# Queries and keys of a cosine attention laid out by feature, normed through TensorE, and fetched per head from DRAM

## The reference, cut to what matters

```python
q = (x @ Wq.T).reshape(b, n, H, 2, DH).transpose(0, 2, 3, 1, 4)   # H = 8, DH = 8
k = (x @ Wk.T).reshape(b, n, H, 2, DH).transpose(0, 2, 3, 1, 4)
v = (x @ Wv.T).reshape(b, n, H, 2 * DH).transpose(0, 2, 1, 3)
L1 = einsum('bhnd,bhmd->bhnm', l2norm(q1), l2norm(k1)) * cos_scale
L2 = einsum('bhnd,bhmd->bhnm', l2norm(q2), l2norm(k2)) * cos_scale
G = tanh(delta_gain * (L1 - L2))
A1, A2 = softmax(L1 + G), softmax(L2 - G)
y = einsum('bhnm,bhmd->bhnd', A1 - lambda_full * A2, v)
```

## Time and profile before

| | us |
|---|---|
| median of 3 runs | 758.65 (756.38 to 758.97) |
| the profiled execution | 760.07 |
| its span, first to last instruction | 758.3 |
| TensorE busy | 664.0 (88%) |
| VectorE busy | 553.7 (73%) |
| ScalarE busy | 479.3 (63%) |
| GpSimd busy | 247.4 (33%) |

### The profile page before, as it was taken

The page is one execution under the profiler, slowest core; times in us unless marked ns, Lnnn a source line. Parts: engine busy times, 40 slices in busy tenths (PEclk is TensorE's granted clock), DMA queues, the critical chain, the costliest instruction groups (busy, mean ns, idle before and its releaser), DMA issues.

```text
span 758.3 us, 9794 instructions
## 1 busy us (share of the span) xinstructions
PE 664.0 (88%) x3514; PEld 287.7 (38%) x3514; DVE 553.7 (73%) x1058; ACT 479.3 (63%) x468; POOL 247.4 (33%) x394
## 2 busy tenths in 40 slices
PE   5999899999999888889988888798898787979795
PEld 2577545444454412222222222132232212547264
DVE  5656430605426389999999999999999997687656
ACT  1243433333342489999999999898999898213211
POOL 3601100102013745951378334547713030020001
PEclk9999999999999979999999999999999999989899
DMA  8000200000000111010111010110011130300430
GB/s 308 3 0 2 85 1 0 1 0 1 0 1 0 28 29 29 15 29 16 29 29 28 18 26 15 29 29 15 18 26 29 28 111 10 105 1 14 98 141 28
DMA packets 16752, 26.00 MB, mean 34 GB/s; under 512 B 2496, under 2 KB 7360, under 8 KB 16320
## 3 DMA queue, kind: packets, MB, share of 16 engines
q1 hardware_dynamic: 16704, 25.38, 12.1%
HBM read 15.87 MB, written 1.11 MB: 22 GB/s over the span
## 4 chain that ended last, share of the span: by engine, by line
PE 45%; ACT 22%; DVE 21%; issue 11%; POOL 1%; DMA 0%; POOLq 0%; DVEq 0%; ACTq 0%
ACT w_hh L881 17%; PE ps L590 7%; PE ps L600 7%; DVE hid L1144 5%; DVE hid L1149 5%; PE ps L630 4%; PE ps L538 4%; PE ps L577 4%; PE ps L519 3%; PE ps L639 3%; PE ps L618 2%; ACT probs L850 2%; PE ps L419 2%; PE ps L450 2%; PE ps L562 1%
## 5 line engine op out<-in xcount | busy, mean ns | idle before, releaser
L881 ACT ACTIVATE w_hh<-hid 128x2048 f32<-128x2048 f32 x128 | 249.0, 1945 | 13.2 <-DVE hid L1149 12.8
L519 PE MATMUL ps<-q_s,k_s 128*128 128x512 bf16 (+1 forms) x512 | 168.6, 393 | 25.6 <-DVE hid L1144 23.9
L538 PE MATMUL ps<-w_hh,v_h 128*32 128x512 f32 x1024 | 140.3, 620 | 31.1 <-ACT w_hh L881 28.6
L1149 DVE SCALAR_TENSOR_TENSOR hid<-ps,probs 128x1024 f32<-128x1024 f32 x86 | 104.6, 1217 | 6.5 <-PE ps L519 5.8
L1144 DVE TENSOR_TENSOR hid<-ps,probs 128x1024 f32<-128x1024 f32 x86 | 104.6, 1216 | 4.4 <-ACT w_hh L881 2.2
L519 PE MATMUL ps<-q_w,k_w 64*128 64x512 bf16 x256 | 100.4, 393 | 1.4 <-DVE hid L1149 1.1
L850 ACT ACTIVATE probs<-ps,gain 128x1024 f32<-128x1024 f32 x86 | 98.5, 1146 | 4.5 <-PE ps L519 4.3
L1479 POOL TENSOR_SCALAR rs<-mv 128x4 f32<-128x4 f32 x32 | 7.3, 227 | 249.6 <-DVE mv L960 249.4
L1053 DVE SCALAR_TENSOR_TENSOR hid<-ps,s_b,rot 128x512 f32<-128x512 f32 x16 | 11.9, 750 | 87.1 <-ACT rot L821 87.1
L519 PEld LDWEIGHTS ps<-q_s,k_s 128*128 128x128 bf16 (+1 forms) x512 | 38.4, 95 | 96.9 <-issue 47.3
L519 PEld LDWEIGHTS ps<-q_w,k_w 64*128 64x128 bf16 x256 | 23.6, 93 | 111.8 <-DVE hid L1149 65.0
(11 more groups left out here) (258 smaller groups left out, 1007.2 us busy)
## 6 DMA issues: line engine op xcount, KB each, us to landing
k_w<-k_s SPq DMA_DIRECT2D x32, 128.0 KB, 2.3
q_w<-q_s SPq DMA_DIRECT2D x32, 128.0 KB, 2.3
w_hh<-w_rows SPq DMA_DIRECT2D x4, 1024.0 KB, 9.0
w_hh<-in_b_h SPq DMA_DIRECT2D x2, 1024.0 KB, 8.8
hid<-w_rows SPq DMA_DIRECT2D x2, 1024.0 KB, 5.9
part<-w_rows SPq DMA_DIRECT2D x8, 256.0 KB, 7.0
x_res<-in_x SPq DMA_DIRECT2D x4, 256.0 KB, 6.0
tab<-in_rope SPq DMA_DIRECT2D x1, 1024.0 KB, 6.8
```

The costliest lines, as they stand in the source:

```text
L519: last = mm(ps[:, base + half, :], k_op[rows, u, keys], q_op[rows, u, half * CHUNK:(half + 1) * CHUNK], start=True, stop=True)
L538: last = mm(ps[VW * g4:VW * g4 + VW, 6, :], v_h[:, u, mt, :], ee[:, mt % 2, g4 * CHUNK:(g4 + 1) * CHUNK], start=(mt == 0), stop=(mt == BT ...
L881: A(ee[:, mt % 2, :], zz[:, mt % 2, :], ACT.Exp).then_inc(S["e"], 1)
L1149: v.scalar_tensor_tensor(zz[:, mt % 2, SEQ:2 * SEQ], banks[:, 4 * CHUNK:6 * CHUNK], -1.0, gg[s % 3], ALU.mult, ALU.subtract).then_inc(S["z ...
```

## The change

Queries and keys are now made with features on partitions: `c_raw` is one product of 512 columns with the weights as the stationary side, for q and for k (L614 of the kernel after), and `c_v` makes v as before (L618). Their norms: GpSimd's squares are multiplied on TensorE with a 128x16 matrix of ones per group of eight (`c_sums`, eight products of 16 columns); VectorE or GpSimd takes the inverse roots and spreads each over its eight features (`spread`); TensorE transposes that (`c_scale`, eight transposes), and the factor, now in PSUM, is multiplied to `raw`. The split in three parts stays.

The parts are written to a DRAM tensor `qk_rows` (`send`, 12 DMAs a chunk), ordered so that the 48 rows of one component of a head lie together; and per head 8 DMAs (`load_head`) bring them to `k_s`, `k_w`, `q_s`, `q_w`, both ways round. This takes the place of the spreading, of the turnings "k" and "q", of their copies and of the crossing. The four head tiles are set to zero once. Chunk 2's projection moves from the start of block C into turnings, chunk 3's pieces are fewer and larger. ScalarE runs one exp of one column before the first tanh of block C. `sg_d` of block D has memory of its own.

```diff
+SPECIAL = {(0, 2): ("raw", 0), (0, 5): ("raw", 1), (1, 1): ("v", 0), (1, 3): ("sums", 0), (2, 1): ("scale", 0),
+           (2, 3): ("scale", 1), (3, 1): ("late turn", 0), (3, 3): ("raw", 2), (3, 5): ("raw", 3), (3, 7): ("v", 1),
+           (4, 5): ("sums", 1), (5, 3): ("scale", 2), (5, 5): ("scale", 3),
...
-    if mt == 0 and n < NH - 1:
-        return ("k", n + 1)
-    if mt == 2 and n < NH - 1:
-        return ("q", n + 1)
...
+Q_PARTS = (0, 0, 1, 0, 2, 1)
+K_PARTS = (0, 1, 0, 2, 0, 1)
...
+        qk_rows = nc.dram_tensor("qk_rows", (BATCH, 2, GROUPS, PARTS, DH, SEQ), BF16, kind="Internal").ap()
...
+        def spread(eng):
+
+            wide = [P, P, DH]
+            return eng.tensor_tensor(sq[:].rearrange("p a (n d) -> p (a n) d", d=DH),
+                                     rstd[:].unsqueeze(2).to_broadcast(wide),
+                                     cs_tab[:].rearrange("p a k h c -> p (a k h c)").unsqueeze(2).to_broadcast(wide), ALU.mult)
...
-            for n in range(NH):
-                for kind, src, dst in (("k", k_s, k_w), ("q", q_s, q_w)):
-                    sp.wait_ge(S["turn_read"], turns_done((kind, n)))
-                    sp.dma_start(dst[high, n % 2, :], src[low, n % 2, :]).then_inc(S["crossed"], 16)
-                    sp.dma_start(dst[low, n % 2, :], src[high, n % 2, :]).then_inc(S["crossed"], 16)
+            def send(c, i):
+                b, half = divmod(c, 2)
+                for a, order in enumerate((Q_PARTS, K_PARTS)):
+                    for seg in range(PARTS):
+                        if order[seg] == i:
+                            sp.dma_start(qk_rows[b, a, :, seg, :, half * CHUNK:(half + 1) * CHUNK],
+                                         part_of(i, c)[:, a, :]).then_inc(S["sent"], 16)
+
+            def load_head(n):
+                b, h = divmod(n, HEADS)
+                for a, own, crossed in ((1, k_s, k_w), (0, q_s, q_w)):
+                    for comp in range(2):
+                        rows = qk_rows[b, a, 2 * h + comp].rearrange("s d t -> (s d) t")
+                        for dst, at in ((own, HALF * comp), (crossed, HALF * (1 - comp))):
+                            sp.dma_start(dst[at:at + ROWS, n % 2, :], rows).then_inc(load[n % 2], 16)
+
+            for c in range(2):
+                sp.wait_ge(S["hi_c"], c + 1)
+                send(c, 0)
+                sp.wait_ge(S["mid_c"], c + 1)
+                send(c, 1)
+                sp.wait_ge(S["lo_c"], c + 1)
+                send(c, 2)
+            sp.wait_ge(S["sent"], 2 * 16 * 2 * PARTS)
+            sp.wait_ge(S["zeroed"], 1)
+            load_head(0)
+            load_head(1)
+            for n in range(2, NH):
+                if n in (4, HEADS - 1):
+                    c = 2 if n == 4 else 3
+                    sp.wait_ge(S["lo_c"], c + 1)
+                    for i in range(3):
+                        send(c, i)
+                if n == HEADS:
+                    sp.wait_ge(S["sent"], 4 * 16 * 2 * PARTS)
+                sp.wait_ge(S["l2"], BT * (n - 1))
+                load_head(n)
...
+            def c_sums(bank):
+                for a in range(2):
+                    for k in range(CT):
+                        o = (a * CT + k) * GROUPS
+                        last = mm(bank[:, o:o + GROUPS], sq[:, a, k * P:(k + 1) * P], grp, start=True, stop=True)
+                return last
...
+                    if c >= 2 and o == 1:
+                        pe.wait_ge(S["fac_c"], c - 1)
+                        for a in range(2):
+                            last = c_scale(a, ps[:, 5 + a, :])
+                        last.then_inc(S["f_c"], 1)
...
+                if 1 <= c < CHUNKS - 1:
+                    pe.wait_ge(S["sq_c"], c)
+                    c_sums(ps[:, 5, :]).then_inc(S["sums_c"], 1)
...
+            pe.wait_ge(load[0], 16 * LOADS)
             c_diff(0, 0, 0)
-            pe.wait_ge(S["crossed"], 64)
             c_first(0, 0, 0)
-            c_prep(CHUNKS - 2)
+            pe.wait_ge(S["yo_b"], CHUNKS)
+            c_second(0, 0, 0)
             c_diff(1, 0, 1)
...
                         if mt3 == 0:
-                            pe.wait_ge(S["turn_read"], turns_done(("q", n3)))
+                            pe.wait_ge(load[n3 % 2], 16 * LOADS * (n3 // 2 + 1))
...
+            me.mark(A(tiny[:, 56:57], tiny[:, 0:1], ACT.Exp))
             tanh_step(0, 0, 0)
-            c_evac_qkv(CHUNKS - 2)
...
+            def c_norms(c):
+                dve.wait_ge(S["sums_c"], c + 1)
+                me.step(v.tensor_scalar(nv[:], ps[:, 5, 0:P], 1e-12, 1e38, ALU.max, ALU.min))
                 rsqrt_start(rstd[:], whole)
+                for _ in range(3):
+                    rsqrt_newton(rstd[:], whole)
+                spread(v).then_inc(S["fac_c"], 1)
...
+            def split(c):
+
+                pool.wait_ge(S["turn_read"], turns_done(("scale", 2 * c - 3)))
+                me.step(g.tensor_scalar(part_of(0, c), sq[:], 1.0, None, ALU.mult))
+                me.step(g.tensor_tensor(raw[:], sq[:], part_of(0, c), ALU.subtract))
+                me.step(g.tensor_scalar(part_of(1, c), raw[:], 1.0, None, ALU.mult))
+                g.tensor_tensor(part_of(2, c), raw[:], part_of(1, c), ALU.subtract).then_inc(S["lo_c"], 1)
```

More of the change, by code:

```diff
@@ L470, in c_turning @@
                 pe.wait_ge(S["turn_read"], turns_done(use) - 1)
[L471 to L476, removed]
+                if kind == "o":
                     pe.wait_ge(S["accout"], i + 1)
@@ L481, in c_turning @@
                     last = turn_chunk(xn_c)
-                elif kind == "late qkv":
-                    last = mm(turn[:, 0:3 * P], xt_c[:, i * P:(i + 1) * P], w_c[:], start=True, stop=True)
+                elif kind == "raw":
+                    if i == 0:
+                        pe.wait_ge(S["xt_c"], CHUNKS - 1)
+                    last = c_raw(i % 2, turn)
+                elif kind == "v":
+                    last = c_v()
+                elif kind == "sums":
+                    pe.wait_ge(S["sq_c"], CHUNKS - 1 + i)
+                    last = c_sums(turn)
+                elif kind == "scale":
+                    pe.wait_ge(S["fac_c"], CHUNKS - 1 + i // 2)
+                    last = c_scale(i % 2, turn)
                 elif kind == "y":
@@ L552, in c_prep_turn, with c_raw, c_v, c_scale @@
                 pe.wait_ge(S["xt_b"], min(c + 3, CHUNKS))
+                if c:
+                    pe.wait_ge(S["vraw_c"], c)
                 turn_chunk(xn_c).then_inc(S["tp_c"], 1)
+            def c_raw(a, bank):
+                return mm(bank, w_c[:, a * P:(a + 1) * P], xt_c[:], start=True, stop=True)
+            def c_v():
+                for k in range(CT):
+                    last = mm(turn[:, k * P:(k + 1) * P], xt_c[:, k * P:(k + 1) * P], w_c[:, 2 * P:3 * P],
+                              start=True, stop=True)
+                return last
+            def c_sums(bank):
+                for a in range(2):
+                    for k in range(CT):
+                        o = (a * CT + k) * GROUPS
+                        last = mm(bank[:, o:o + GROUPS], sq[:, a, k * P:(k + 1) * P], grp, start=True, stop=True)
+                return last
+            def c_scale(a, bank):
+                for k in range(CT):
+                    last = nc.tensor.transpose(bank[:, k * P:(k + 1) * P], sq[:, a, k * P:(k + 1) * P], ident[:])
+                return last
             def c_prep(c):
@@ L558, in c_prep @@
                     pe.wait_ge(ld["cw"], 64)
[L559 to L563, removed]
+                if c:
+                    pe.wait_ge(S["qh_c"], c)
+                for a in range(2):
+                    c_raw(a, ps[:, 5 + a, :]).then_inc(S["qkv_c"], 1)
+                c_v().then_inc(S["qkv_c"], 1)
             pe.wait_ge(S["y_a"], TILES)
@@ L1323, in _ @@
                         b_stats(CHUNKS - 1)
-                    if at == (0, 4):
-                        c_sums(CHUNKS - 2)
+                    if use and use[0] == "sums":
+                        dve.wait_ge(S["turn_read"], turns_done(use))
+                        rsqrt_start(rstd[:], whole)
                         dve.sem_inc(S["rs_c"], 1)
```

227 lines of the change are left out of this document (95 added, 132 removed).

## The result

| | before | after |
|---|---|---|
| median, us | 757.67 (756.27 to 758.97, 16 runs) | 760.43 (758.3 to 761.09, 16 runs) |
| profiled execution / span, us | 760.07 / 758.3 | 760.38 / 758.5 |

The ratio is 1.003, 95% interval 1.0021 to 1.0038: 2.3 us slower (1.6 to 2.9), inside the 0.5% that the prediction called no change. Three stretches make it up. Each is counted from its own first instruction, since the first loads and block A end up to 1.9 us apart from one execution to the next.

The account below looks back on a forecast made before the run. No engine bounds the whole: TensorE limits block B, ScalarE block C, with VectorE behind in some heads. Block B +7.1, start of block C -3.3, its loop -4.1 and clock +1.0 sum to +0.7: 759.3 us, range 752 to 768.

Parts of the forecast that it names:

- waits for the factor: Block B, first layer of chunks 2 and 3: TensorE idles 2.5 and 1.4 us until the factor is ready, together +3.9.
- turnings gone: Block B: the two turnings before head 0, 0.61 each less drain, are removed from TensorE, -0.9 us.
- projection: Block B: bigger pieces without waits for ScalarE's copies make 2.6 against 3.11 us a chunk, twice 0.5, -1.0.
- start of block C: First c_diff to first exp: 6.4 us in place of 9.75, table loaded earlier and projection moved away, -3.3.
- head 0, reductions gone: Block C, head 0: 1024-column reductions become a read of 128 columns, so it loses 2.0 of its 3.5 us excess.
- heads 1 to 5, reductions and new sums: Block C: sums on TensorE let twice 0.5 us through, +1.0; head 5's start loses 0.6 of 0.9.
- head 7's rows: Block C: split, 20 DMA issues at 0.50 and landing make head 7's c_diff late by 1.3 us; 2 taken.
- heads 9 to 15, copies gone: Block C: k and q copies off VectorE gain where it is behind, at most 5.3 plus 0.6; 4.5 us taken.
- clock: TensorE's half clock after new waits, notably chunk 2's 2.5 us hole: +1.0 us for all, between 0 and 5.
- rival with half clock in both holes: Clock falls in both block B holes and at block C's start, 2 us each: 764.3; chance 0.13.
- queue rival: SyncE's 20 DMAs at 0.9 us each make heads 7 and 4 late: 770; decides from 0.65 an issue; chance 0.18.
- large-relief rival: Relief 10 in place of 7.1, sums hidden, head 7 in time, clock holds: -6.2 us, 752.5; chance 0.19.

Follow-up runs that it names:

- e5: Kernel after with factor wait one group later and chunk 3's sends behind head 7's loads, plus 30 unused VectorE reductions standing for k/q copies: 756.3 us, ratio 0.9984.
- e1: Kernel after with the factor waited for after three output groups of the layer, not two, and ScalarE's two split copies a group later: 755.08 us, ratio 0.9958.
- e4: Kernel before with only the exp of one column added ahead of its first tanh: 755.29 us, ratio 0.9961 to before.
- e7: Kernel after with factor wait one group later and chunk 3's sends behind head 7's loads, but without the one-column exp: 752.66 us, ratio 0.9939.
- e9: Kernel after with 24 unused transposes filling TensorE's first hole ahead of the factor wait in block B: 760.05 us, ratio 1.0031.
- e6: Kernel after with factor wait one group later and chunk 3's sends behind head 7's loads, plus twelve unused GpSimd copies per head from the third: 751.9 us, ratio 0.9927.
- e10: Kernel after run again unchanged, as the measure beside the run with the first hole filled: 760.25 us, ratio 1.0032.

## Why the prediction was right

The kernel was forecast at 759.3, 0.7 us above before, and came at 760.43, 2.3 us above: no change within 0.5%, for the reason given, gains and costs of one size in different blocks. That the sum came so near is in part luck, since errors of the terms cancel. Term by term, from the profiled executions:

| step of the prediction | predicted | measured |
|---|---|---|
| group sums, two chunks | +3.4 | +3.4 |
| scale transposes, two chunks | +1.7 | +2.0 (1.06 and 0.93) |
| waits for the factor | +2.5, +1.4 | +2.6, +1.45 |
| turnings gone | -0.9 | -0.6 |
| projection | -1.0 | -0.5 |
| start of block C | -3.3 | -3.3 |
| head 0, reductions gone | -2.0 | -2.5 |
| heads 1 to 5, reductions and new sums | +0.4 | +0.6 |
| head 7's rows | +2.0 | +3.6 |
| heads 9 to 15, copies gone | -4.5 | -5.9, of which `e5` gives 3.7 to the copies |
| clock | +1.0 | +1.5 behind the first hole |

*Waits for the factor.* The reckoning from VectorE's list held to 0.1. `e1` shows that they were on the path in full: moved by one output group they vanish, and with them the clock's loss.

*Turnings.* The price of 0.9 was wrong in part. The one inside the second layer is gone in full, 0.45. The one behind it had stood between the second layer and the output product, which waits for the last gelu (`e_g2_b`); from the end of the second layer to the first `c_diff` it is 4.51 before and 4.38 after, so of its 0.45 only 0.13 was won. Most of it had lain in that wait, under cover that the prediction did not look for.

*Start of block C.* The 3.3 came out as reckoned. Of it 1.4 is the table load, by `e4` and `e7`; the rest is the projection and its copies, which no run took out by itself.

*Head 0.* In before one exp of head 0 waits 1.47 us behind the `z_second` that follows the reduction of 1024 columns, and the next starts 0.96 late too; both gaps are gone in after. That is read from the traces, and no run tests it alone.

*Projection.* Half of what was counted. The 2.71 of each chunk is near the estimate of 2.6, but it stands against 2.95 of its share before, not 3.11, whose last piece drained beside the next product.

*Clock.* The 1.0 was for everything. Behind the first hole alone it was 1.5, by `e9`. The fall at the start of block C was there before and stays (0.51 from 270 to 275), inside the other terms. The rival with half clock in both holes falls: the second, of 1.3 us, left the clock at 1.00.

*Head 7.* The chain was right link by link, but for one price: from the split's start to the first send 10.1 (10.05 forecast), landing 2.46 (2.3). The 20 issues took 11.5 and not 10.0, as a send takes 0.63 and a load 0.465. The trace of before had a hint: of most pairs of crossing DMAs the second takes 0.60, and the prediction took the first one's 0.46 for all. Counted as the prediction does, from the exp of (5, 6) at 403.18, the `c_diff` of head 7 had to start at 423.88 and started at 426.54: late by 2.7 rather than 1.3. The restart cost 0.9 more in the next step, with the clock at 0.71. The queue rival puts its point at 0.65 an issue; with 0.575 on average it was not reached, and head 4 was in time.

*Copies.* 5.9 in place of 4.5 in heads 9 to 15. `e5` puts two such instructions a head back and loses 4.9 in the loop, 3.7 of it in heads 9 to 14. So 3.7 of the 5.9 are shown to be VectorE's copies. The other 2.2 stay open: 1.3 of them are in head 14, which scatters by 1, and the transposes that went from TensorE with the copies were not put back by any run. The large-relief rival put its relief, copies and reductions together, at 10 in place of 7.1; it measured 8.6 (5.9, head 0's 2.5, 0.2 at head 5), between the two. The rival falls by its other terms: head 7 was late and the clock fell. That GpSimd's spreading was free fits `e6` but isn't shown to better than 3 us.

Block B came out 2.0 above its 7.1 and the clock's 1.0, and that is where the 1.6 between forecast and result come from; in the loop the errors of head 7 (1.6) and of the copies (1.4) cancel, which is luck. What the prediction did not see is that both new waits can be taken out by moving a few statements. Then the change is worth 7 to 8 us, of which the layout itself has 4 to 5.

## What to carry to other kernels

Where a change comes out even, sum its gains and its waits apart: two waits worth 9.6 us hid a gain of 7 to 8 here, and each went by moving one wait or one group of DMAs to where its data is ready anyway. Try each part of a change on the kernel before as well: one exp of one column made some 2 to 3 of those 7 to 8 us, and needs nothing of the rest. A wait in a stretch where TensorE is full costs its idle time and can cost a slower clock behind it, as the longer of the two did here, so look at the granted clock of the 5 us behind every new hole. In a queue of DMAs in order, put loads that somebody waits for ahead of stores that nobody needs yet.

## What the runs showed of the hardware

- A hole of 2.44 us in otherwise full TensorE work was followed by a clock of 0.66 over 5 us and cost 1.5 us more; one of 1.27 us was followed by 1.00. With 24 transposes in the first hole the clock stayed at 1.00. In `e9` an idle time of 3.94 us was followed by 0.50, in after one of 3.15 by 0.71.
- SyncE issued the 12 stores from SBUF to DRAM ahead of head 7, 128 KB each in the order of `qk_rows`, every 0.63 us, and the loads of 96 KB behind them every 0.465; the first load took 0.59. The last load of head 7 landed 2.3 (`e10`), 2.5 (after) and 3.2 us (`e9`) after its issue.
- Eight products of 16 columns with a 128x128 float32 stationary side take 1.70 us, 0.21 each, at full clock. The router's eight of 8 columns take 1.71 (690.04 to 691.75 in before), and `c_v`'s four of 128 columns 0.89 (167.86 to 168.75 in after), 0.22 each: up to 128 columns the narrow side hardly matters.
